# VectorE's order within a pair of heads: pieces of the two layers ahead of the row maxima and of the addition to y

## The reference, cut to what matters

```python
x = x + 0.5 * ffn(layernorm(x))
x = x + attn(layernorm(x))            # 16 heads of 64, softmax over 512 keys, then a norm of its own
x = x + 0.5 * ffn(layernorm(x))

def ffn(x):                           # I = 352
    gate, up = fp4_linear(x, w_gate), fp4_linear(x, w_up)
    return fp4_linear(silu(gate) * up, w_down)

def fp4_linear(x, w):                 # blocks of 16 are scaled by max/6 and rounded to 8 magnitudes
    return einsum('bsk,nk->bsn', fp4_quant_dequant(x), fp4_quant_dequant(w))
```

## Time and profile before

| what | value |
|---|---|
| runs | 2251.21, 2252.6, 2254.46 us; median 2252.6 |
| the profiled execution | 2249.3 us, its span 2247.5 us |
| busy in the span | PE 94%, DVE 71%, POOL 64%, ACT 52% |
| granted TensorE clock, mean | 0.982 |

### The profile page before, as it was taken

One profiled execution on the slowest core, in us unless ns is written; L12 is line 12 of the kernel. 1 busy time (PEld: TensorE's weight loads), 2 busy tenths in 40 slices (PEclk: granted clock), 3 DMA queues, 4 the chain that ended last, 5 costly groups with the idle time before them and its releaser, 6 DMA issues.

```text
span 2247.5 us, 39655 instructions
## 1 busy us (share of the span) xinstructions
PE 2103.3 (94%) x15049; PEld 1173.3 (52%) x15049; DVE 1605.0 (71%) x2627; ACT 1158.0 (52%) x1767; POOL 1427.2 (64%) x1289
## 2 busy tenths in 40 slices
PE   3999999999999999999999999999999999999984
PEld 2455555555555555555555555555555555555543
DVE  6675778777687777868777676877768777676643
ACT  2455555545555454555555455554554545455432
POOL 3365666757576675857657576675757667585652
PEclk8899999999999999999999999999999999999996
DMA  1000000000000000000000000000000000000000
GB/s 60 1 7 2 7 2 2 12 2 7 7 7 7 2 11 2 7 7 6 8 2 12 2 7 7 2 12 2 7 7 6 7 2 11 2 3 7 2 7 10
DMA packets 167498, 15.91 MB, mean 7 GB/s; under 512 B 148304, under 2 KB 166928, under 8 KB 167312
## 3 DMA queue, kind: packets, MB, share of 16 engines
q1 hardware_dynamic: 167312, 13.39, 5.1%
HBM read 7.03 MB, written 4.19 MB: 5 GB/s over the span
## 4 chain that ended last, share of the span: by engine, by line
PE 70%; DVE 17%; issue 4%; ACT 3%; SPq 2%; POOL 2%; DMA 1%; POOLq 0%; DVEq 0%
PE pS L957 18%; PE pO L985 14%; PE pX L1009 5%; PE pM L1095 4%; DVE nmax L810 4%; PE pX L969 4%; PE pO L941 4%; PE pM L941 3%; PE pM L997 3%; PE FpF L332 2%; PE LpF L332 2%; SPq L575 2%; PE FpF L295 2%; DVE ON L899 2%; PE LpF L308 2%
## 5 line engine op out<-in xcount | busy, mean ns | idle before, releaser
L683 POOL TENSOR_TENSOR ES<-ES,E 128x512 f32<-128x512 f32 x512 | 666.5, 1323 | 305.7 <-ACT E L760 303.1
L810 DVE TENSOR_REDUCE nmax<-pX 128x2 fp32r<-128x1024 f32 x512 | 623.3, 1217 | 240.0 <-PE pX L969 234.5
L760 ACT ACTIVATE E<-pS 128x1024 f32<-128x1024 f32 x512 | 523.8, 1023 | 518.9 <-PE pS L957 516.7
L985 PE MATMUL pO<-E,VA 128*64 128x512 f32 x2048 | 524.3, 611 | 5.9 <-DVE KL L911 5.8
L677 POOL TENSOR_TENSOR ES<-E 128x512 f32<-128x512 f32 x256 | 323.3, 1283 | 257.1 <-ACT E L760 257.1
L969 PE MATMUL pX<-KH,QH 64*128 64x512 f32 x1024 | 247.9, 424 | 21.7 <-DVE nmax L810 15.1
L957 PE MATMUL pS<-QH,KH 64*128 64x512 f32 x1024 | 253.9, 492 | 10.0 <-ACT E L760 10.0
L969 PEld LDWEIGHTS pX<-KH,QH 64*128 64x128 f32 x1024 | 187.7, 306 | 61.3 <-DVE nmax L810 27.4
L957 PEld LDWEIGHTS pS<-QH,KH 64*128 64x128 f32 x1024 | 95.9, 183 | 225.9 <-issue 220.1
L985 PEld LDWEIGHTS pO<-E,VA 128*64 128x64 f32 x2048 | 116.2, 135 | 172.3 <-issue 172.3
L957 PE MATMUL pS<-SH,onesr 64*128 64x512 f32 x1024 | 203.7, 393 | 0.0
(11 more groups left out here) (190 smaller groups left out, 3723.7 us busy)
## 6 DMA issues: line engine op xcount, KB each, us to landing
RROW<-RC SPq DMA_DIRECT2D x512, 2.0 KB, 2.0
xin<-in_L_attn_x SPq DMA_DIRECT2D x16, 256.0 KB, 2.9
SH<-nmax SPq DMA_DIRECT2D x256, 2.0 KB, 2.0
LC<-LROW SPq DMA_DIRECT2D x256, 2.0 KB, 2.1
out<-X SPq DMA_DIRECT2D x16, 256.0 KB, 2.5
E<-in_L_attn_w_q SPq DMA_DIRECT2D x1, 512.0 KB, 4.2
E<-in_L_attn_w_k SPq DMA_DIRECT2D x1, 512.0 KB, 5.3
wv<-in_L_attn_w_v SPq DMA_DIRECT2D x1, 512.0 KB, 7.1
```

The source lines that it names most:

```text
L683: ins = g.tensor_tensor(ES[i % 3][:, hd, :], ES[i % 3][:, hd, :], E[s][:, hd, :], ALU.add)
L760: a.activation(E[s][:, :, :], pS[:, :, :], ACT.Exp).then_inc(s_exp, 1)
L810: v.tensor_reduce(nmax[px % 2][:, :, t:t + 1], pX[:, :, :], AX.X, ALU.max, negate=True).then_inc(s_max, 1)
L985: ins = pe_.matmul(pO[half(hd), :], VA[of][:, kt, j * 128 + 64 * hd:j * 128 + 64 * hd + 64], E[kt][:, hd, :], start=kt == 0, stop=kt == KT ...
```

## The change

DVE's `body` is written in another order; no operation is added, removed or altered, and the programs of the other engines are the same. At s = 0, 2 and 3 the other pieces now stand right behind the PSUM pieces and ahead of the maxima; before, they stood at the step's end. At s = 3 the normalization ON is issued last; before, it was first. At s = 1 the other pieces stay behind maxima, QL and KL, but now come ahead of the addition to y.

```diff
--- before.py
+++ after.py
@@ -893,16 +893,19 @@
                         if s == 0 and p % 2 == 1 and there(i - 2, NP):
                             dve.wait_ge(s_lc, 64 * (i // 2))
                             v.reciprocal(REC[:, :, :], LC[:, :, :]).then_inc(s_rec, 1)
+                        first_ffn_psum(b, t)
+                        last_ffn_psum(b, t)
+                        if s != 1:
+                            first_ffn(b, t)
+                            last_ffn(b, t)
+                        if s < 2:
+                            maxima(i + 1, p + 1, s + 2)
+                        else:
+                            maxima(i + 2, p, s - 2)
                         if s == 3 and there(i - 3, NP):
                             dve.wait_ge(s_rb, i - 2)
                             wait(dve, s_proj, (i - 3) // 2)
                             v.tensor_tensor(ON[(p - 3) % 2][:, :], OT[(i - 3) % 3][:, :], pM[:, :], ALU.mult).then_inc(s_norm, 1)
-                        first_ffn_psum(b, t)
-                        last_ffn_psum(b, t)
-                        if s < 2:
-                            maxima(i + 1, p + 1, s + 2)
-                        else:
-                            maxima(i + 2, p, s - 2)
                         if s == 1 and there(i + 2, NP):
                             dve.wait_ge(s_qhi, i + 3)
                             v.scalar_tensor_tensor(QL[(i + 2) % 3][:, :], pM[:, :], SCALE, QH[(i + 2) % 3][:, :].bitcast(F32),
@@ -910,14 +913,15 @@
                             dve.wait_ge(s_khi, i + 3)
                             v.scalar_tensor_tensor(KL[(i + 2) % 3][:, :], pO[:, :], 1.0, KH[(i + 2) % 3][:, :].bitcast(F32),
                                                    ALU.mult, ALU.subtract).then_inc(s_klo, 1)
+                        if s == 1:
+                            first_ffn(b, t)
+                            last_ffn(b, t)
                         if s == 1 and p % 2 == 1 and there(i - 4, NP):
                             bo, yp = (b, bpar) if p >= 4 else (b - 1, 1 - bpar)
                             dve.wait_ge(s_proj, (i - 3) // 2)
                             dve.wait_ge(s_y0, bo + 1)
                             wait(dve, s_yacc, (i - 5) // 2)
                             v.tensor_tensor(Yacc[yp][:, :], pX[:, 0, :], Yacc[yp][:, :], ALU.add).then_inc(s_yacc, 1)
-                        first_ffn(b, t)
-                        last_ffn(b, t)
                 steps(dve, body)
 
             @block.tensor
```

## The result

The changed kernel takes 2314.1 us (median of 4 runs, 2312.3 to 2316.9), the kernel before 2251.9 us (2250.5 to 2254.5) on the same chip. The ratio is 1.0276, with a 95% interval of 1.0258 to 1.0294. The forecast was 2294 us in a range of 2262 to 2332. The profiled executions took 2312.3 us (span 2310.5) and 2249.3 us (span 2247.5): 63.0 us more.

A forecast was written before the change was run, and what follows sets the result against it. PE was taken to set the time, busy 129.50 of 133.60 us a batch. The terms summed to 3.0 us a batch, 39 us in 13 batches, 42 us together, giving 2294 us in a range of 2262 to 2332.

The forecast's parts named there:

- b = 1: Batch 1, with no L pieces at t = 3 to 6: +0.9 us in all.
- the taking of turns: Rival: POOL's additions come first at C, D and E (1.5, 1.6, 1.3 us); 2330 us, chance 0.19.
- C: t = 6: L max_h ahead of the maxima makes pX late, +0.8 us a batch, between bounds 0 and 1.5.
- only what the order forces: Rival: C, D, E at 0, G at 1.1, H at 0.7; 1.0 us a batch, 2269 us, chance 0.15.
- D: t = 10: F max_h ahead of the maxima delays pX, +0.4 us a batch, at worst +1.6.
- E: t = 11: F round_h ahead of the maxima, its wait for Fmag moving along, delays pX, +0.5 us a batch.
- A: t = 3: ON behind L max_h and the maxima holds PE's V product, +1.8 us a batch.
- B: t = 5: rounding ahead of Yacc makes PE's pX late, +0.3 us a batch.
- G: t = 13: F round_h ahead of Yacc makes PE's pX late, +1.3 us a batch.
- c: PE's wait for POOL's rescale (step t = 13) goes, -0.62 us a batch.
- H: t = 14 and 15: moments now ahead of the maxima of t = 14, not those of t = 15; -0.6 us a batch.
- t = 31: The rounding of t = 30 starts earlier, so the wait on L's gate goes, -0.36 us a batch.

The follow-up runs named there:

- e5: The changed kernel with POOL's second and third addition of a pair cut to 16 of 512 columns; 2285.8 us, ratio 1.0152.
- e2: The kernel before, with only ON moved behind the maxima in every pair; 2243.0 us, ratio 0.9959.
- e7: The kernel before, with only the other pieces at s = 0, 2 and 3 moved ahead of the maxima; 2357.0 us, ratio 1.0464.
- e4: The kernel before, with only the other pieces at s = 1 moved ahead of Yacc; 2288.8 us, ratio 1.0162.
- e1: The changed kernel with ON put back to the front of s = 3; 2330.0 us, ratio 1.0342.
- e9: e4 with four useless 128x512 products on PE ahead of pX at t = 14, in b = 2 to 14; 2270.0 us, ratio 1.0080.

## Why the prediction was right, term by term

The mechanism held: in a loop where PE is busy 97% of the time, DVE's own waits are no room for a piece that is longer than the wait, and PE stopped at the places that the prediction named. The forecast came out 20 us short: about 11 of them lie in the terms of the batch, 3.4 in the falls of the clock, 2.4 in b = 1, and most of the rest ahead of the first exponential, where executions scatter. Neither of the two nearest rivals fits: the taking of turns would have had C too, and with POOL's additions short 34 of the 62 us stay (e5); with only what the order forces D and E would be 0. By the terms:

- **A was right, slightly small**: 2.03 for 1.8. The "0.2 to 0.3 without L max_h in front" was wrong: e2 measured 1.22. I had let the maxima start as soon as the PSUM pieces were done, without asking when PE has their pX ready: 0.73 us later, in e2. The same 0.73 hides half of L max_h, so in the full A the error nearly cancels. It doesn't in b = 1, which has no L max_h at t = 3: that step loses 1.23 us there, and the forecast had no A for b = 1 at all (it had B's 0.3, though b = 1 has no L piece at t = 5 either, and t = 6 didn't move).
- **B and G were right**: 0.46 and 1.47 for 0.3 and 1.3. At t = 5 rounding and Yacc ran unhindered; at t = 13 the first rounding operation took 1.33 us instead of 0.88. PE went on 0.1 us behind Yacc.
- **C failed**: its 0.8 is not there, t = 7 is -0.76 and in e2, without pieces, -0.58. The forecast took the middle between no hindrance and a scale that sits out both of POOL's additions. At t = 6 the trace after shows on POOL, and then on DVE:

```profile
1046.98 2.55 POOL L683 TENSOR_TENSOR ES<-ES,E 128x512 f32<-128x512 f32 x2 [3.40 <-ACT E L760]
```

```profile
1047.73 0.57 DVE L201 TENSOR_SCALAR Lqh_tie<-Lqh_amax 128x44 f32<-128x44 f32 x1
1048.22 0.17 DVE L202 TENSOR_SCALAR Lqh_scale<-Lqh_amax 128x44 f32<-128x44 f32 x1
```

  The tie is held until about the middle of POOL's pair (1048.26), and the scale gets through there, before the second addition holds anything: 0.4 us, within the slack.

- **D was mis-sized, and is the largest error**: 1.41 for 0.4, near its upper end of 1.6. I had chosen the value near the hindrance of the row of before, in which the tie came when the first addition was nearly over. As F max_h went ahead of the maxima, the tie came right behind the start of POOL's pair, and tie and scale took one addition each. e5 shows that this is all of D. The Trainium skill, page "SBUF — State Buffer", section "Who interferes with whom", says that a DVE instruction with two SBUF inputs, or in a two-port mode, and a GpSimd instruction that reads SBUF lock each other out; here the trace agrees with such a lock (1.23 and 1.32 beside full additions, 0.19 and 0.18 beside short ones). At t = 6 only the tie was held. So the rival of taking turns was right at one place of its three (D), wrong at C, and at E nearer than the forecast.
- **E was mis-sized**: 0.96 for 0.5. In the changed kernel the rounding starts behind the late maxima and takes 0.87 + 1.84 us beside POOL's additions; by an estimate with the 0.89 us for each operation of e5, the maxima would end near 1069.2, and PE is ready for pX at 1069.6. The wait for Fmag, with which the forecast started E, is not there, since D has made PE and the maxima late; it comes back only in e5, with 0.57.
- **c, H and t = 31 were right**: -0.50, -0.65 and -0.58 for -0.62, -0.6 and -0.36. H came as two steps, +0.57 at t = 15 and -1.22 at t = 16; e5 shows that the first is POOL's doing too.
- **Not in the sum**: the falls of the clock (3.4 us in all), and most of b = 1, with 3.3 instead of 0.9: half of that is the 1.23 at t = 3.

The sum is 3.84 instead of 3.0 a batch. C's 0.8, which didn't come, has covered nearly all of what D lacked; without this accident the forecast would have been another 10 us short.

The prediction treated the change as a list of places. e7 shows what that leaves out: taken alone the pieces ahead of the maxima cost 105 us, and the other two parts of the change give 43 of that back, since the rounding ahead of Yacc runs in a wait and frees DVE for the piece of the next step, ON behind the maxima frees it at t = 4 and 12, and the clock falls 2 times instead of 8.

## What to carry to other kernels

On an engine that works in order, a wait is room for another piece only if everything queued behind that piece still ends before the bottleneck asks for it; take the gap to each such consumer from the timeline and compare it with the piece. Split a reorder into its parts and its places before it is kept or thrown away: of this change, ON behind the maxima in seven pairs of eight gives 2225 us, 1.2% under the kernel before (2222 with REC early at one place), where the whole costs 2.8%. The parts have to be measured together, too, since their sum here was twice what the whole cost.

## What the runs showed of the hardware

A wait of PE can cost more than its length. After waits of 2.29 us in e4 the granted clock stood at 0.50 for a stretch of 3.4 us in 12 batches of 13, and the products of L989 took 2.59 instead of 1.94 us; after waits of 1.81 us in the changed kernel it happened in 2 of 13, in e7 after 7 of 12 waits of 1.8 us; after the 14 waits of 1.0 us for ON in e2, and in the kernel before, whose longest wait between 150 and 2050 us is 1.0, never. The length of one wait doesn't decide it alone: two of e1's ten falls, at t = 21, had no wait above 1.0 us in front, and one wait of 2.46 us in e7 had no fall behind it. Four products that nobody reads, put into the wait, kept the clock up (e9) and took 19 us off e4.

The other surprise is how much a tiny operation can wait: 44 numbers per partition took 1.2 to 1.3 us beside POOL's additions of 128x512 and 0.18 beside additions of 128x16, and POOL's pair grew from 2.51 to 3.80 us where DVE's rounding ran beside it.
